# Three transposes of normalized rows moved from TensorE and ScalarE to one DMA each, in a hybrid attention and expert kernel planned anew

## What is computed

```
x = x + attention(layernorm(x))       # 16 query heads, 4 key groups, head size 16, causal, RMS norm and rotation of q and k
x = x + experts(layernorm(x))         # router, 2 of 8 experts for each row, silu(g) * u of width 176
x = x + memory(layernorm(x))          # elu(q)+1 against 4 memory banks, mixed with softmax weights
x = x + experts(layernorm(x))         # the same expert layer again
```

## Time and profile before

| | |
|---|---|
| median of 3 runs | 576.04 us |
| profiled execution, first to last instruction (span) | 531.0 us |
| what lies around the span, from the two lines above | 45.0 us |
| TensorE busy | 485.2 us, 91% of the span |
| VectorE busy | 374.1 us, 70% |
| ScalarE busy | 269.3 us, 51% |
| GpSimd busy | 249.9 us, 47% |

### The profile page before, as it was taken

The page is one execution under the profiler, slowest core; times in us unless marked ns, Lnnn a source line. Parts: engine busy times, 40 slices in busy tenths (PEclk is TensorE's granted clock), DMA queues, the critical chain, the costliest instruction groups (busy, mean ns, idle before and its releaser), DMA issues.

```text
span 531.0 us, 10990 instructions
## 1 busy us (share of the span) xinstructions
PE 485.2 (91%) x3380; PEld 328.7 (62%) x3380; DVE 374.1 (70%) x1098; ACT 269.3 (51%) x642; POOL 249.9 (47%) x308
## 2 busy tenths in 40 slices
PE   7998999999999999899999989999979999899960
PEld 3545665765765676676676635675848776677740
DVE  5999989889999866754445557868777766344473
ACT  4577898887887874333333414533223543334320
POOL 5519339148650152473324655347372857343330
PEclk9999999999999999999999979999989999999995
DMA  6563700111130422464335492011133266433485
GB/s 202 202 265 139 175 21 12 51 58 46 61 101 2 131 101 71 130 191 129 108 93 169 84 174 40 0 61 61 60 95 95 105 194 193 123 98 114 163 287 171
DMA packets 43737, 60.77 MB, mean 114 GB/s; under 512 B 5857, under 2 KB 38241, under 8 KB 43041
## 3 DMA queue, kind: packets, MB, share of 16 engines
q1 hardware_dynamic: 33152, 37.72, 23.3%
q0 software_dynamic: 9984, 21.83, 13.7%
q10 hardware_dynamic: 544, 0.52, 0.3%
HBM read 28.89 MB, written 25.00 MB: 101 GB/s over the span
## 4 chain that ended last, share of the span: by engine, by line
PE 61%; DVE 9%; DMA 4%; issue 3%; ACT 3%; SPq 1%; POOL 1%; POOLq 0%; DVEq 0%; ACTq 0%
PE PS L1148 16%; PE PS L1165 10%; PE PS L1194 4%; PE PS L1035 4%; PE PS L1157 3%; PE PS L1012 3%; PE PS L1203 3%; PE PS L1129 3%; PE PS L1097 2%; PE PS L1211 2%; PE PS L1175 2%; DMA kbd<-ys 2%; PE PS L1086 2%; DVE smax L1490 2%; PE PS L1053 2%
## 5 line engine op out<-in xcount | busy, mean ns | idle before, releaser
L1889 POOL DMA_INDIRECT ys<-yo,xin x78 | 75.9, 973 | 103.8 <-DVE yo L1711 94.1
L1148 PE MATMUL PS<-wexp,xTt 128*128 x312 | 105.2, 464 | 2.9 <-issue 1.7
L1490 DVE TENSOR_REDUCE smax<-PS 128x1 f32<-128x512 f32 (+3 forms) x176 | 102.2, 632 | 6.2 <-PE PS L1014 5.7
L1316 ACT ACTIVATE prob<-PS 128x512 f16<-128x512 f32 (+1 forms) x176 | 92.7, 562 | 20.3 <-PE PS L1037 18.5
L1874 POOL DMA_INDIRECT xs<-xn,pos x64 | 62.5, 976 | 57.9 <-DVE pos L1585 40.9
L1165 PE MATMUL PS<-wexp,hT 88*128 x312 | 80.4, 384 | 2.5 <-ACT hT L1366 2.2
L1148 PEld LDWEIGHTS PS<-wexp,xTt 128*128 128x128 f32 x312 | 54.7, 190 | 25.2 <-issue 5.5
L1698 DVE SCALAR_TENSOR_TENSOR sg<-th,PS 128x176 f32<-128x176 f32 x78 | 26.2, 336 | 59.0 <-ACT th L1360 58.7
L1360 ACT ACTIVATE th<-PS 128x176 f32<-128x176 f32 x78 | 24.7, 317 | 82.6 <-PE PS L1148 82.6
L1165 PEld LDWEIGHTS PS<-wexp,hT 88*128 88x128 f32 x312 | 55.4, 189 | 15.3 <-issue 4.5
L1035 PE MATMUL PS<-qT,kbd 128*128 128x512 f16 (+3 forms) x256 | 60.8, 299 | 2.2 <-ACT qT L1308 1.0
(11 more groups left out here) (210 smaller groups left out, 849.0 us busy)
## 6 DMA issues: line engine op xcount, KB each, us to landing
xin<-xs SPq DMA_DIRECT2D x78, 129.0 KB, 2.2
wexp<-in_experts SPq DMA_DIRECT2D x4, 1216.0 KB, 9.8
kbd<-ys SPq DMA_DIRECT2D x18, 256.0 KB, 4.4
xs<-zeros SPq DMA_DIRECT2D x32, 129.0 KB
xn<-xn SPq DMA_DIRECT2D x8, 512.0 KB, 3.3
xall<-ys POOLq DMA_DIRECT2D x6, 512.0 KB, 6.8
out<-xall SPq DMA_DIRECT2D x8, 256.0 KB, 2.8
kbd<-kT SPq DMA_DIRECT2D x60, 32.0 KB, 1.9
```

Of the source, the lines that this page charges most:

```text
L1148: mm = pe.matmul(PS[:, bank, 0:2 * FI], xTt[:, j % NXT, kc * P:(kc + 1) * P], wexp[:, bass.ds(expert[f, j], 1), kc * 2 * FI:(kc + 1) * 2 * FI]
L1316: act.activation(prob[:, u % NPR, 0:nr * w], PS[:, bank, 0:nr * w], ACT.Exp, scale=ATT_SCALE)\
L1490: dve.tensor_reduce(smax[:, i, REP * g + r0:REP * g + r0 + nr], PS[:, bank, 0:nr * w].rearrange("p (r w) -> p r w", r=nr), AX.X, ALU.max). ...
L1889: pool.indirect_dma_start(ys[f], bass.IndirectOffsetOnAxis(xin[:, j % NXIN, D + 1:D + 2].bitcast(I32), axis=0), yo[:, j % NYO], None).then ...
```

## The change

Batches 1 to 3 get a step `f_turn b` on SyncE: one DMA that transposes all of `xh` into `xhT`, issued when the four `f_apply` of the batch and the last `qkv` of the batch before are done. `qkv b 0` on TensorE waits for the landing (`xh_turned`), and so does `f_apply b+1 0`, which writes `xh` again. The 24 transposes on TensorE and the three copies on ScalarE are gone. Batch 0 stays as it was. `xhT` is laid out by tile and then by half. The planner has new costs for many steps, VectorE's `shift` and `normalize` steps must follow each other in order, the filler matmuls at the start have other settings, and the table `NUDGE` is another, of 180 entries where it had 52, so all five lists are new.

```diff
--- before.py
+++ after.py
@@ -91,17 +91,43 @@
 
 
...
 
...
+NUDGE = {("add", 0): 34, ("apply", 0): 104.2, ("apply", 1): 1.9, ("bank_shift",): 8.8, ("banks",): 334.5,
...
+         ("queries", 1): -12.1, ("queries", 2): -64.6, ("queries", 3): 1, ("queriesT", 0): 40.1,
...
@@ -109,7 +135,7 @@
...
-    WARM_FROM, WARM_RISE, WARM_UNTIL, WARM_GAP, WARM_STEP = 3.2, 10.0, 25.0, 0.4, (0.25, 0.16)
+    WARM_FROM, WARM_RISE, WARM_UNTIL, WARM_GAP, WARM_STEP = 3.05, 9.0, 25.0, 0.4, (0.32, 0.16)
...
@@ -238,37 +264,39 @@
     for i in range(NT):
         a = applies(b, i)
         w.add(a, r(), 0.49 if a == ACTE else 0.35, "f_apply", b, i, after=[(DVE, "f_scale", b) if a == ACTE else (root, "f_pow", b)]
-              + [(PE, "f_turn", b - 1, h) for h in range(len(halves(b - 1))) if b]
+              + ([(SP, "f_turn", b - 1)] if b > 1 else [(PE, "f_turn", 0, h) for h in range(2)] if b else [])
               + [(a, "f_apply", b, i - 1)] * (i > 0 and applies(b, i - 1) == a))
-    for h, (i0, i1) in enumerate(halves(b)):
+    if b:
+        w.add(SP, r(), 0.5, "f_turn", b, after=[(applies(b, i), "f_apply", b, i) for i in range(NT)] + [(PE, "qkv", b - 1, NT - 1)], lands=4.0)
+    for h, (i0, i1) in enumerate(halves(b) if b == 0 else ()):
         w.add(PE, r(), 0.113 * (i1 - i0), "f_turn", b, h, after=[(applies(b, i1 - 1), "f_apply", b, i1 - 1), (DVE, "constants")],
               banks=m, emptied=(DVE if h else ACTE, "f_turn", b, h))
         w.add(DVE if h else ACTE, r(), 0.92 if b else 0.5, "f_turn", b, h, after=[(PE, "f_turn", b, h)] + [(PE, "qkv", b - 1, NT - 1)] * (b > 0))
     for i in range(NT):
-        w.add(PE, r(), 0.69, "qkv", b, i, after=[(DVE if h else ACTE, "f_turn", b, h) for h in range(len(halves(b)))]
+        w.add(PE, r(), 0.69, "qkv", b, i, after=([(SP, "f_turn", b)] if b else [(DVE if h else ACTE, "f_turn", b, h) for h in range(2)])
               + [(ACTE, "constants"), (POOL, "bias"), (POOL, "presets")]
               + [(PE, "qkv", b, i - 1)] * (i > 0), banks=m, emptied=(ACTE, "v", b, i))
         w.add(ACTE, r(), 0.35, "qkv", b, i, after=[(PE, "qkv", b, i)] + [(ACTE, "qkv", b, i - 1)] * (i > 0)
               + [(p0, "queries", b - 1, p) for p in range(2) if b > 0 and i == 0])
     for i in range(NT):
-        w.add(ACTE, r(), 0.2, "v", b, i, after=[(ACTE, "qkv", b, i)])
+        w.add(ACTE, r(), 0.11, "v", b, i, after=[(ACTE, "qkv", b, i)])
...
@@ -649,7 +678,7 @@
-        xhT = sb("xhT", [P, KC, S], F16)
+        xhT = sb("xhT", [P, NT, KC, P], F16)
...
@@ -746,7 +775,7 @@
-        qk_ready = sem("qk_ready")
+        qk_ready, xh_turned = sem("qk_ready"), sem("xh_turned")
...
@@ -873,6 +902,12 @@
                     elif kind == "load_experts":
                         for e in range(0, NE, 2):
                             sp.dma_start(wexp[:, e:e + 2], experts[:, e:e + 2]).then_inc(experts_loaded, 16)
+                    elif kind == "f_turn":
+                        (b,) = a
+                        normalized(sp, b)
+                        made(sp, "qkv", b - 1, NT - 1)
+                        sp.dma_start_transpose(xhT[:].rearrange("p i k s -> p (i k) s"), xh[:].rearrange("p i c -> p (i c)"))\
+                          .then_inc(xh_turned, 16)
...
@@ -944,11 +979,8 @@
                     elif kind == "f_turn":
                         b, h = a
                         i0, i1 = halves(b)[h]
-                        if b == 0:
-                            pe.wait_ge(ident_ready, 1)
-                            pe.wait_ge(xh_ready[h], 1)
-                        else:
-                            normalized(pe, b)
+                        pe.wait_ge(ident_ready, 1)
+                        pe.wait_ge(xh_ready[h], 1)
                         bank = room(pe, kind, b, h)
                         for i in range(i0, i1):
                             for kc in range(KC):
@@ -957,16 +989,18 @@
                         mm.then_inc(filled[bank], 1)
                     elif kind == "qkv":
                         b, i = a
-                        for h, (i0, _) in enumerate(halves(b)):
-                            if i == i0:
+                        for h, (i0, _) in enumerate(halves(0)):
+                            if b == 0 and i == i0:
                                 out_of(pe, "f_turn", b, h)
+                        if b and i == 0:
+                            pe.wait_ge(xh_turned, 16 * b)
...
                         bank = room(pe, kind, b, i)
                         for kc in range(KC):
-                            pe.matmul(PS[:, bank, 0:QKV], xhT[:, kc, i * P:(i + 1) * P], wqkv_h[:, kc],
+                            pe.matmul(PS[:, bank, 0:QKV], xhT[:, i, kc], wqkv_h[:, kc],
...
@@ -1244,9 +1278,11 @@
                         b, i = a
                         if i == 0:
                             act.wait_ge(f_nb_ready, b + 1)
-                            if b:
-                                for h in range(len(halves(b - 1))):
-                                    made(act, "f_turn", b - 1, h)
+                            if b == 1:
+                                for h in range(len(halves(0))):
+                                    made(act, "f_turn", 0, h)
+                            elif b:
+                                act.wait_ge(xh_turned, 16 * (b - 1))
...
@@ -1255,10 +1291,8 @@
                         b, h = a
                         i0, i1 = halves(b)[h]
                         bank = made(act, kind, b, h)
-                        if b:
-                            made(act, "qkv", b - 1, NT - 1)
-                        act.activation(xhT[:, :, i0 * P:i1 * P], bank16(bank)[:, 0:KC * (i1 - i0) * P]
-                                       .rearrange("p (k s) -> p k s", k=KC), ACT.Copy).then_inc(taken[bank], 1)
+                        act.activation(xhT[:, i0:i1].rearrange("p i k s -> p k i s"), bank16(bank)[:, 0:KC * (i1 - i0) * P]
+                                       .rearrange("p (k i s) -> p k i s", k=KC, i=i1 - i0), ACT.Copy).then_inc(taken[bank], 1)
...
-                        dve.tensor_copy(xhT[:, :, i0 * P:i1 * P], bank16(bank)[:, 0:KC * (i1 - i0) * P]
-                                        .rearrange("p (k s) -> p k s", k=KC)).then_inc(taken[bank], 1)
+                        dve.tensor_copy(xhT[:, i0:i1].rearrange("p i k s -> p k i s"), bank16(bank)[:, 0:KC * (i1 - i0) * P]
+                                        .rearrange("p (k i s) -> p k i s", k=KC, i=i1 - i0)).then_inc(taken[bank], 1)
```

More of the change, by code:

```diff
@@ L240, in front @@
               + ([(POOL if b > 1 else ACTE, "f_pow", b - 1), (DVE, "queries", 0, 1)] if b else []))
-    w.add(root, r(), 1.03 if b else 0.48, "f_pow", b, after=[(DVE, "f_stats", b, 0), (DVE, "f_stats", b, 1)]
+    w.add(root, r(), 1.03 if b else 0.6, "f_pow", b, after=[(DVE, "f_stats", b, 0), (DVE, "f_stats", b, 1)]
           + [(applies(b - 1, i), "f_apply", b - 1, i) for i in range(NT) if b])
@@ L279, in front @@
                 for a in (ACTE, DVE):
-                    w.add(a, r(), 1.0, "place_keys", after=[(PE, "keysT" if a == ACTE else "first_keysT", *[b] * (a == ACTE)),
+                    w.add(a, r(), 1.2 if a == ACTE else 0.88, "place_keys", after=[(PE, "keysT" if a == ACTE else "first_keysT", *[b] * (a == ACTE)),
                                                             (POOL, "presets")])
@@ L323, in scores @@
         t = unit(BU * b + NU * (g + 1) - 0.5)
-        w.add(DVE, t, 0.47, "shift", b, g, after=[(DVE, "first", b, g, n) for n in range(NU)])
+        w.add(DVE, t, 0.5, "shift", b, g, after=[(DVE, "first", b, g, n) for n in range(NU)],
+              behind=[(DVE, "shift", *divmod(NG * b + g - 1, NG))] * (b + g > 0))
         last = NG * b + g - 2
@@ L330, in scores @@
         w.add(DVE, unit(BU * b + NU * (g + 2) + LAG), 0.65, "normalize", b, g, after=[(PE, "values", b, g, NU - 1)]
-              + [(PE, "outT", b - 1)] * (b > 0 and g == 0))
+              + [(PE, "outT", b - 1)] * (b > 0 and g == 0), behind=[(DVE, "normalize", *divmod(NG * b + g - 1, NG))] * (b + g > 0))
 def divmod_unit(u):
@@ L395, in route @@
           emptied=(DVE, "top2", f, b))
-    w.add(DVE, r(), 1.3, "top2", f, b, after=[(PE, "router", f, b)] + prior)
+    w.add(DVE, r(), 1.4, "top2", f, b, after=[(PE, "router", f, b)] + prior)
     w.add(ACTE, r(), 0.1, "choose", f, b, after=[(DVE, "top2", f, b)])
     w.add(DVE, r(), 0.55, "choose", f, b, after=[(DVE, "top2", f, b), (SP, "load_late")])
-    w.add(PE, r(), 0.17, "rank", f, b, after=[(DVE, "choose", f, b)], banks=banks, emptied=(DVE, "place", f, b))
+    w.add(PE, r(), 0.12, "rank", f, b, after=[(DVE, "choose", f, b)], banks=banks, emptied=(DVE, "place", f, b))
     w.add(DVE, r(), 0.57, "weigh", f, b, after=[(ACTE, "choose", f, b), (DVE, "choose", f, b)])
@@ L412, in release @@
     prior = [(DVE, "plan", f, n - 1, 3)] if n else [(DVE, "down", f - 1, TILES - 1)] if f else [(DVE, "presets")]
```

(6 more changed lines are left out.)

62 lines of the change are left out of this document (43 added, 19 removed).

## The result

The changed kernel takes 580.14 us (median of 20 runs, 576.97 to 586.54), the kernel before 577.63 us (20 runs beside them). The ratio is 1.0056, with an interval of 1.0031 to 1.0081: slower, by about 3.2 us. I had said 587, that is +1.9%. The direction is right, the time is inside my range, the size is not.

What follows compares the result with a forecast made beforehand. TensorE was taken as busy 485.2 of 531.0 us, with no engine having room from 38.8 to 185. Terms +9.6, +4.1, -0.9, +2.5, -3.7 gave +11.6: span 542.6, plus 45.0 is 587.6, said as 587; range 573 to 594.

Steps and rivals of the forecast that it cites:

- The queue order: SyncE's queue: batch 1's transposing DMA, issued at 32.7 us, waits for the weights' data until 45.9 and lands at 48.4.
- Rival 1: Batch 1's transpose isn't held by the weights, lands within some 4 us of 32.7; nothing stops, 573.5 us; 16%.
- rival 2: Batch 1's transpose is slow in itself, eight pieces in a row, landing 10 to 15 us behind 45.9; 595 to 600; 10%.
- The stop and its price: TensorE from about 36 us, all three engines from 39, stand still until 48.4; the span grows by 11.6 us.
- The landing term: TensorE resumes at 48.4 us, when batch 1's transpose lands, instead of 38.8: +9.6 us.
- The clock term: After the stop TensorE's clock drops to 1.2 GHz for 3.5 to 6.9 us, half of it lost: +2.5 us.
- my 3.7: Slack: half of TensorE's 7.4 us of idle time from 38.8 to 185 us takes up part of the shift: -3.7.
- my 4.1: TensorE work done by 38.8 us before but still owed in the new list, `qkv` 2.7 and other 1.4: +4.1 us.
- The transposes that go away: TensorE saves 0.44 us a batch, 1.3 for three, 0.9 of it counted; ScalarE's 3.1 us of copies given nothing.
- Transposes 2 and 3: SyncE's transposing DMAs of batches 2 and 3 cost nothing, as long as each lands within some 5 us.
- From 185 us on: Expert and memory steps behind the attention keep nearly the same order: given nothing, 1 us either way for the range.
- Rival 3: The stop comes but the new plan's orders win it back, or the weights' data leave gaps: within 0.5%; 6%.

Runs made afterwards that it cites:

- new lists: Changed kernel's order and banks everywhere, but the three moved transposes given back to TensorE and ScalarE: 571.4 us, 0.9886 of the kernel before.
- transpose first: Changed kernel with batch 1's transposing DMA ahead of the expert weight loads on SyncE: 522.29 us, 0.9826 of the kernel before; again on another chip 569.94 us, 0.9847.
- late lists old: Changed kernel with batch 1's transposing DMA ahead of the weights, but the kernel before's order and banks behind batch 3's last `project`: 578.8 us, 1.0017 of the kernel before.

## Why the prediction was right in its direction and wrong in its size

- **The queue order.** Right. I had put the landing at 48.4: weights landed by 45.9, 2.5 more. It was 45.1: the loads were issued 1.0 us earlier than in the kernel before, their last packet ended at 43.6, the transpose's packets followed without a gap and took 1.4. Half the weights ahead gave 8.7 us, none 4.4 or less. Rival 1 (not held) and rival 2 (slow in itself) both fell: with nothing ahead of it the transpose needs 3.1 to 4.7 us. The estimate from the Trainium skill's page VectorE: DVE Perf Modes (The three transpose paths), its figure for one block taken eight times in a row, was 10.5; the trace does not bear it out.
- **The stop and its price.** The mechanism is right: 9.26 us of waiting, VectorE dry for 8 us, half clock until 52 us. The forecast sum of +11.6 is 12.5 without the 0.9 for the transposes; taking the stop away gave 11.5 (12.7 by the ratios 1.0067 and 0.9847 on two chips). That they agree so well is in part luck. The landing term was 3.3 us too large (45.1 for 48.4). The clock term was a little small: TensorE was busy for 6.4 us at half clock, an estimated loss of 3.2 where I took 2.5. With both put right the 12.5 would be 9.9, so less slack was given back than my 3.7, or more work was owed than my 4.1; no run tells which.
- **The transposes that go away.** I counted 1.3 us. The runs show 1.5 (new lists against transpose first) and can't tell it from nothing.
- **Transposes 2 and 3.** Right: 3.5 and 3.8 us, no wait of note.
- **"From 185 us on, the expert and memory steps stand in nearly the same order as before; I give that nothing and take 1 us either way."** This is the step that failed. The changed lists there, which I priced at nothing, are worth a ratio of 0.9892 and 0.9884 by themselves, 6.2 us, the better half of it between 313 and 405 us. With them, 11.5 less 6.2 less the 1.5 of the transposes is 3.8; with the 8.9 us that the lists are worth behind transpose first it is 11.5 less 8.9, 2.6. Measured were 3.2. The premise was wrong too: 318 of TensorE's 400 steps there stand at another place, if only by 2 on average. My own had a 5.30 us stretch with TensorE busy for 2.27 in it, at a wait of 3.0 us that the new lists cut to 1.0. Rival 3 ("the new plan's orders win it back", 6%) was the right mechanism for at least half the cost.
- **"The runs' median is 45.0 us more, and I add these 45.0 unchanged."** Wrong as a statement: 1.8 us lies around the span, the rest is another kind of chip. It moved the forecast by little: the gain from transpose first is about the same part of the time on both kinds (0.9826 and 0.9847). What the stop costs was only measured on the slower kind.
- **The chances.** Half of rival 1 and all of rival 3 are 0.14, not the 0.12 that I put within 0.5%; with the 0.03 the other half is 0.11, not 0.14. It changes nothing in the forecast.

What stays open: how much the three DMA transposes give by themselves (0.9847 against 0.9886, each with an interval of some 0.0046 either way), and why the new lists within the attention give nothing (late lists old, 1.0017) although they are made for them. The changed late lists were only tried without the stop ahead of them; that they save as much behind it is taken from the sum above and not shown.

## What to carry to other kernels

A small DMA on whose landing the tensor engine waits belongs ahead of a bulk load and not behind it, and a second queue was no way round it here: moved by one place it turned a loss of 0.6% into a gain of 1.5 to 1.7%, faster than both kernels. When a change comes with a new order of everything, price the order by itself: keep the finished lists and swap them in parts, since planning again with one thing undone gives other lists, and read the two traces' waits by stretch before giving "nearly the same order" nothing. And don't count one shortened wait as a gain before it is timed: here it came back as two.

## What the runs showed of the hardware that was not expected

- Two DMAs on two queues share by packet, not by byte: from 37 to 43 us 275 packets of 256 bytes started beside 242 of 9728 bytes. All 1024 small ones took 9.9 us, and 1.4 us alone. The landing on the second queue took 15.6 us, on the same queue behind the weights 13.4.
- A transposing DMA of 256 KB within SBUF lands 3.1 to 4.7 us after its issue begins when no weights are ahead of it; of these its packets take 1.4 us. Its issue holds SyncE 1.23 to 2.19 us, against 0.63 for a key DMA (7.61 us for twelve).
- Chips differ by 9% for one program: the kernel before took 532 us in two sets of runs and 578 to 580 in three. The mean granted clock in the traces was 0.98 on the faster kind and 0.93 to 0.94 on the slower. On the slower ones PE, ACT and DVE show joint stops of 2 to 9 us (the longest 8.8) whose releaser is no work of the kernel; what they are stays open. The ratios carry over: transpose first is 0.9826 on one kind and 0.9847 on the other.
